# Feed-forward products on two halves of the tensor engine's rows, with the two tiles of a pair changing places

## The reference, cut to what matters

```
x = x + attention(layernorm(x), ctx)                  # 1st part of the program
n = layernorm(x)                                      # over the last axis
w_scale = mean(abs(weight))
q_w = sign(weight) * (abs(weight) > 0.5 * w_scale)    # -1, 0, 1
i_scale = max(abs(n)) / 127                           # over all of n
q_n = clip(round(n / i_scale), -128, 127)
x = x + (q_n @ q_w.T * w_scale * i_scale + bias)      # 2nd part of the program
```

## Time and profile before

| | |
|---|---|
| Time, median of 3 runs | 1268.88 us (1268.54 to 1269.37) |
| Profiled execution, own time | 1268.9 us |
| Its span, first to last instruction | 1267.0 us |
| PE busy over the span | 1201.2 us (95%) |
| DVE busy | 1124.7 us (89%) |
| ACT busy | 1001.1 us (79%) |
| Mean granted TensorE clock | 0.991 |
| Bytes read and written in HBM | 137.11 and 122.64 MB |

### The profile page before, as it was taken

How to read it: one execution, slowest core, us unless ns; L and a number is a source line. 1 busy time by engine, 2 the same in 40 slices (tenths; PEclk the granted TensorE clock), 3 DMA queues, 4 the chain that set the end, 5 groups by cost and what they waited for, 6 DMA issues and landing times.

```text
span 1267.0 us, 42077 instructions
## 1 busy us (share of the span) xinstructions
PE 1201.2 (95%) x12408; PEld 983.0 (78%) x12471; DVE 1124.7 (89%) x2410; ACT 1001.1 (79%) x2339; POOL 794.2 (63%) x1536
## 2 busy tenths in 40 slices
PE   7999999999999999999999999999789999999997
PEld 7998888888888888888888888888645555555554
DVE  4656999999999999999999999999878888888887
ACT  4566888888888888888888888888768888888886
POOL 4767898898998988989989889899700000000000
PEclk9999999999999999999999999999889999999999
DMA  9772555555555555555555543323029999999945
GB/s 291 225 205 66 160 178 169 173 173 170 164 178 166 178 168 175 170 174 162 182 163 181 164 123 94 87 84 84 2 99 398 403 396 398 399 408 396 395 206 212
DMA packets 97241, 260.26 MB, mean 205 GB/s; under 512 B 42538, under 2 KB 53994, under 8 KB 76723
## 3 DMA queue, kind: packets, MB, share of 16 engines
q1 hardware_dynamic: 97154, 259.75, 59.6%
q10 hardware_dynamic: 48, 0.07, 0.0%
HBM read 137.11 MB, written 122.64 MB: 205 GB/s over the span
## 4 chain that ended last, share of the span: by engine, by line
DVE 44%; PE 35%; issue 15%; DVEq 3%; ACT 1%; POOL 1%; DMA 0%; SPq 0%; POOLq 0%; ACTq 0%
DVE amax L903 10%; PE pT_ps L1265 10%; PE sc_ps L1265 9%; DVE x_sb L940 8%; DVE mx_sb L918 7%; DVE bn_sb L930 6%; DVE e_sb L922 6%; PE qo_ps L1069 5%; PE xT_ps L1256 5%; DVE bn_sb L910 3%; PE sc_ps L1263 2%; DVE mv_sb L947 2%; DVE rinv_sb L890 2%; PE xT_ps L1058 1%; PE pT_ps L1263 1%
## 5 line engine op out<-in xcount | busy, mean ns | idle before, releaser
L1210 PE MATMUL qo_ps<-wqs,xT_sb 128*128 128x128 f32 x2048 | 262.6, 281 | 0.9 <-ACT xT_sb L700 0.9
L1210 PEld LDWEIGHTS qo_ps<-wqs,xT_sb 128*128 128x128 f32 x2048 | 238.2, 191 | 21.5 <-issue 20.0
L1233 PEld LDWEIGHTS pT_ps<-v_blk,pT_sb 103*128 103x128 f32 x1536 | 197.3, 190 | 11.8 <-ACT pT_sb L712 0.9
L940 DVE SCALAR_TENSOR_TENSOR x_sb<-x_sb,mv_sb,xT_ps 128x512 f32 (+1 forms) x256 | 180.0, 745 | 25.5 <-DVE bn_sb L930 10.8
L1233 PE MATMUL pT_ps<-v_blk,pT_sb 103*128 103x136 f32 x1536 | 200.1, 280 | 0.3 <-ACT pT_sb L712 0.3
L1008 DVE TENSOR_TENSOR x_sb<-x_sb 128x512 f32 (+1 forms) x256 | 164.7, 684 | 1.2 <-ACT x_sb L758 1.2
L700 ACT ACTIVATE xT_sb<-xT_ps 128x512 f32<-128x512 f32 x256 | 139.1, 595 | 33.3 <-PE xT_ps L1136 28.9
L663 ACT ACTIVATE sq_sb<-x_sb 128x512 bf16 (+1 forms) x256 | 162.4, 634 | 0.6 <-DVE x_sb L940 0.2
L903 DVE TENSOR_REDUCE amax<-x_sb (+1 forms) x128 | 154.6, 1208 | 0.3 <-issue 0.3
L758 ACT ACTIVATE x_sb<-pT_ps,mean,cols 128x512 f32<-128x512 f32 x128 | 99.5, 777 | 63.6 <-PE pT_ps L1265 63.6
L1265 PE MATMUL pT_ps<-wT,x_sb 128*128 128x512 f16 x512 | 131.4, 379 | 3.2
(11 more groups left out here) (135 smaller groups left out, 2673.7 us busy)
## 6 DMA issues: line engine op xcount, KB each, us to landing
out_y<-x_sb SPq DMA_DIRECT2D x112, 1024.0 KB, 6.5
x_sb<-in_x SPq DMA_DIRECT2D x128, 512.0 KB, 3.9
x_sb<-out_y SPq DMA_DIRECT2D x48, 1024.0 KB, 8.9
x_sb<-in_ctx SPq DMA_DIRECT2D x38, 256.0 KB, 4.0
k_blk<-k_scr SPq DMA_DIRECT2D x256, 9.6 KB, 1.7
v_scr<-x_sb SPq DMA_DIRECT2D x38, 68.0 KB, 3.0
k_scr<-x_sb SPq DMA_DIRECT2D x38, 64.0 KB, 3.3
v_blk<-v_scr SPq DMA_DIRECT2D x128, 10.2 KB
```

Source lines behind the costliest of these rows:

```text
L940: dve.scalar_tensor_tensor(out=x1_at(kj, gj, t), in0=x_sb[:, kj // 2, 2 * (kj % 2) + t, :], scalar=mv_sb[:, kj, t, 0:1], in1=bank[t][:, :] ...
L1210: last = pe.matmul(bank[2][:, t * HD:(t + 1) * HD], xT_sb[:, t, c, :], wqs[:, c, :], start=c == 0, stop=c == EC - 1)
L1233: last = pe.matmul(bank[6][:, t * HEADS * VC:(t + 1) * HEADS * VC], pT_sb[0:CR, t, c * P:(c + 1) * P], v_blk[0:CR, slot, c, :, :].rearrang ...
```

## The change

PE's 128 rows are used as two halves, rows 0 to 63 (n = 0) and rows 64 to 127 (n = 1), through the feed-forward part.

- `q_T(j, m)` makes sixteen transposes of 64 rows in place of eight of 128; those of half n go to bank 2m + n. `unoffset` reads the two banks with one instruction of the same size.
- `ffn(j, m, second)` works on the pair. At first (`second` = 0) half n = 0 works on tile 2m and half n = 1 on tile 2m + 1: two bias products of 64 rows, then for each of the four chunks c one product for each half. Then (`second` = 1) the tiles change places, and the other half of the rows is added to each. Between the two, PE waits for its own first part (`ffn_half`), so that two halves never add into one bank at a time.
- `batch(j)` now runs `ffn(j, 0, 0)`, `q_T(j + 1, 0)`, `ffn(j, 0, 1)`, `ffn(j, 1, 0)`, `q_T(j + 1, 1)`, `ffn(j, 1, 1)`. The transposes stand between the two parts of a pair.
- Both tiles of a pair are done at once: `ffn_done` counts pairs, and ACT waits for it before the pair's first tile. The orders of ACT and DVE stay.
- The bias rows are copied to rows 64 to 72 by two more DVE instructions before `bias_ready`; the wait for `quant_01` and `quant_23` is on a counting register.

```diff
             def scale_out(g, k, back):
                 j = g * XS + k
                 for t in range(TPB):
-                    act.wait_ge(ffn_done_t, 4 * j + t + 1)
+                    if t % 2 == 0:
+                        act.wait_ge(ffn_done, 2 * j + t // 2 + 1)
...
-            dve.tensor_scalar(bones[0:BR, :], ones_sb[0:BR, :], row, None, ALU.mult).then_inc(bias_ready, 1)
+            mids(dve.tensor_scalar(bones[0:BR, :], ones_sb[0:BR, :], row, None, ALU.mult))
+            dve.tensor_copy(brow[HALF:HALF + BR, :], brow[0:BR, :])
+            dve.tensor_copy(bones[HALF:HALF + BR, :], bones[0:BR, :]).then_inc(bias_ready, 1)
...
-                at_least(dve, ffn_done_t, 4 * j + 2 * m - 2)
+                at_least(dve, ffn_done, 2 * j + m - 1)
...
             def q_T(j, m):
-                pe.wait_ge(quant_23 if m else quant_01, 2 * j + 2)
                 at_least(pe, qT2_copied, 2 * j + m - 1)
+                held(quant_23 if m else quant_01, 2 * j + 2, q23_count if m else q01_count, 2)
                 for t in range(2):
                     for c in range(EC):
-                        q16 = qm_sb[:, m, t, c * P:(c + 1) * P].bitcast(F16)
-                        at0 = (t * E + c * P) // 2
-                        last = pe.transpose(bank[m][:, at0:at0 + P // 2].bitcast(F16), q16[:, ::2], ident16[:, :])
+                        for n in range(2):
+                            lo, hi, at0 = n * HALF, (n + 1) * HALF, (t * EC + c) * HALF // 2
+                            q16 = qm_sb[lo:hi, m, t, c * P:(c + 1) * P].bitcast(F16)
+                            last = pe.transpose(bank[2 * m + n][:, at0:at0 + HALF // 2].bitcast(F16), q16[:, ::2],
+                                                ident16[lo:hi, lo:hi])
                 last.then_inc(qT2_done, 1)
-            def ffn(j, t):
...
+            def ffn(j, m, second):
+                if second:
+                    pe.wait_ge(ffn_half, 4 * j + 2 * m + 2)
+                else:
+                    at_least(pe, scaled_t, 4 * j + 2 * m - 2)
+                    pe.wait_ge(qT2_copied, 2 * j + m + 1)
+                    for n in range(2):
+                        rows = slice(n * HALF, (n + 1) * HALF)
+                        pe.matmul(bank[4 + 2 * m + n][:, :], bones[rows, :], brow[rows, :], start=True, stop=False)
                 for c in range(EC):
-                    last = pe.matmul(bank[4 + t][:, :], q16T_sb[:, t, c, :], wT[:, c, :], start=False,
-                                     stop=c == EC - 1)
-                last.then_inc(ffn_done_t, 1)
+                    for n in range(2):
+                        rows, t = slice(n * HALF, (n + 1) * HALF), 2 * m + (n ^ second)
+                        last = pe.matmul(bank[4 + t][:, :], q16T_sb[rows, t, c, :], wT[rows, c, :], start=False,
+                                         stop=second == 1 and c == EC - 1)
+                        if c == EC - 1 and not second:
+                            last.then_inc(ffn_half, 1)
+                if second:
+                    last.then_inc(ffn_done, 1)
...
             def batch(j, more=True):
                 for m in range(2):
-                    for t in range(2):
-                        ffn(j, 2 * m + t)
+                    ffn(j, m, 0)
                     if more:
                         q_T(j + 1, m)
+                    ffn(j, m, 1)
```

More of the change, by code:

```diff
@@ L281, in build @@
                              "scale_ready", "bias_ready"))
-        quant_01, quant_23, qT2_done, qT2_copied, ffn_done_t, scaled_t, sum_done_t = (
-            sem(n) for n in ("quant_01", "quant_23", "qT2_done", "qT2_copied", "ffn_done_t", "scaled_t", "sum_done_t"))
+        quant_01, quant_23, qT2_done, qT2_copied, ffn_half, ffn_done, scaled_t, sum_done_t = (
+            sem(n) for n in ("quant_01", "quant_23", "qT2_done", "qT2_copied", "ffn_half", "ffn_done", "scaled_t", "sum_done_t"))
         def at_least(eng, s, n):
@@ L991, in _ @@
                                           op0=ALU.mult, op1=ALU.add))
-            dve.tensor_scalar(bones[0:BR, :], ones_sb[0:BR, :], row, None, ALU.mult).then_inc(bias_ready, 1)
+            mids(dve.tensor_scalar(bones[0:BR, :], ones_sb[0:BR, :], row, None, ALU.mult))
+            dve.tensor_copy(brow[HALF:HALF + BR, :], brow[0:BR, :])
+            dve.tensor_copy(bones[HALF:HALF + BR, :], bones[0:BR, :]).then_inc(bias_ready, 1)
             def unoffset(j, m):
                 dve.wait_ge(qT2_done, 2 * j + m + 1)
-                at_least(dve, ffn_done_t, 4 * j + 2 * m - 2)
-                dve.tensor_scalar(q16T_sb[:, 2 * m:2 * m + 2, :, :],
-                                  bank[m][:, :].bitcast(F16).rearrange("p (t c r) -> p t c r", t=2, c=EC),
+                at_least(dve, ffn_done, 2 * j + m - 1)
+                ps = (xT_ps, qo_ps)[m]
+                dve.tensor_scalar(q16T_sb[:, 2 * m:2 * m + 2, :, :].rearrange("p t c (n r) -> p (t c) n r", n=2),
+                                  ps[:, :, 0:E // 2].bitcast(F16).rearrange("p n (b r) -> p b n r", r=HALF),
                                   -HALF_OFFSET, None, ALU.add).then_inc(qT2_copied, 1)
@@ L1246, in _ @@
               .then_inc(scale_row, 1)
+            q01_count, q23_count = pe.alloc_register("q01_count"), pe.alloc_register("q23_count")
+            pe.reg_mov(q01_count, 6)
+            pe.reg_mov(q23_count, 6)
             def q_T(j, m):
-                pe.wait_ge(quant_23 if m else quant_01, 2 * j + 2)
                 at_least(pe, qT2_copied, 2 * j + m - 1)
+                held(quant_23 if m else quant_01, 2 * j + 2, q23_count if m else q01_count, 2)
                 for t in range(2):
                     for c in range(EC):
-                        q16 = qm_sb[:, m, t, c * P:(c + 1) * P].bitcast(F16)
-                        at0 = (t * E + c * P) // 2
-                        last = pe.transpose(bank[m][:, at0:at0 + P // 2].bitcast(F16), q16[:, ::2], ident16[:, :])
@@ L1257, in q_T @@
-                last.then_inc(qT2_done, 1)
-            def ffn(j, t):
-                pe.wait_ge(qT2_copied, 2 * j + t // 2 + 1)
-                at_least(pe, scaled_t, 4 * j + t - 3)
-                pe.matmul(bank[4 + t][:, :], bones[:, :], brow[:, :], start=True, stop=False)
-                for c in range(EC):
-                    last = pe.matmul(bank[4 + t][:, :], q16T_sb[:, t, c, :], wT[:, c, :], start=False,
-                                     stop=c == EC - 1)
-                last.then_inc(ffn_done_t, 1)
+                        for n in range(2):
[3 more added lines that the diff above has]
+                                                ident16[lo:hi, lo:hi])
```

## The result

The changed kernel takes 1363.04 us (median of 4 runs, 1362.09 to 1364.62) against 1268.89 us before (1268.54 to 1269.37): ratio 1.0743, 95% interval 1.0724 to 1.0762. The forecast was 1382 us in a range of 1340 to 1440. The span of the profiled execution is 1362.8 us, its mean granted clock 0.981.

A forecast was written before the change was run, and what follows sets the result against it. PE was taken to bound the feed-forward part at 5.21 us a batch, then a loop through ACT at 7.01. 1268.9 + 111.6 (62 batches) + 1.1 = 1381.6, said as 1382 us, range 1340 to 1440.

The forecast's parts named there:

- S: PE's second half-products of a tile pair in the feed-forward part: four pairs of products, forecast 0.864 us.
- F: PE's first half-products of a tile pair in the feed-forward part: five pairs with the bias, forecast 1.08 us.
- Rival C: Feed-forward products: halves don't run side by side for 16-bit products of 512 columns; +174 us, 1556 us; chance 0.03.
- step 1: PE's feed-forward products: halves in different banks run side by side, 0.216 us a pair; a tile pair 1.94 us, before 2.16.
- The loop over ACT: Feed-forward batches 1 to 62: PE's products, ACT's two scalings and two quantises, PE's transposes in a ring, 7.01 us a batch.
- S1: PE's second half-products of pair 1 in a batch, forecast 0.864 us; ACT's scaling waits for them.
- Q0: PE's transposes of the next batch's pair 0, forecast 0.52 us; they wait for ACT's quantise.
- step 2: PE's feed-forward transposes: sixteen of 64 rows at 0.0325 us each, 0.52 us a group, before 0.445; bounds 0.22 and 0.90.
- Q: One group of sixteen 64-row transposes on PE for a pair of the next batch, forecast 0.52 us.
- rival B: PE's clock falls in the loop's waits: +80 us if one batch in three, +239 in all; over 50 us, chance 0.09.
- Rival A: PE's transposes: weight loads in a line, 0.90 us a group, 47 us more, 1429 us; chance 0.07.
- D: Feed-forward part: PE stays the bound at 4.93 us a batch, so faster, 1251 us; chance 0.04.

The follow-up runs named there:

- e7: Kernel before with only ACT's order altered, quantising between tiles 1 and 2 for the batch after next: 1268.73 us, ratio 0.9999.
- e1: Changed kernel with only ACT's order altered, quantising between tiles 1 and 2 for the batch after next: 1252.50 us, ratio to before 0.9878.
- e2: Changed kernel with the transposes put back behind the pair's last product, halves kept: 1304.37 us, ratio to before 1.0284.
- e6: e1's kernel with whole 128-row transposes and the unoffset of before, products still by halves: 1270.43 us, ratio to before 1.0015.
- e3: Kernel before with only the transposes made by halves (changed q_T and unoffset, old ffn): 1283.61 us, ratio to before 1.0119.

## Why the prediction was right, and where not

- PE bound the part before: e7 agrees (no gain from ACT's order alone). The 0.31 us to spare for ACT are read from the rows of before; no run tests them.
- Halves run side by side (0.216 us for a pair): right for 16-bit products of 512 columns, 0.87 us for S and 1.08 for F. Rival C (no side by side) did not come. In step 1 the rows of L1233 that I compared with as "full" have 103 rows, not 128.
- The loop over ACT is the new bound: right, and shown by e1 and e2. Its place, its 62 turns, and PE's 2 us wait in each (2.1 forecast) were as written. PE's busy share is 68% and not the 73% that I wrote: my own terms give 4.93 of 7.01 us, 70%.
- The loop's length was 6.60 us at the full clock in ACT's loop, for 7.01. Term by term, measured for forecast: S1's end to ACT 0.40 for 0.31; two scalings and two quantises 2.67 for 2.70; ACT's end to Q0 0.24 for 0.15; products 2.81 for 2.81; the two groups of transposes 0.49 for 1.04. The step that was mis-sized is step 2: Q at 0.0325 us a transpose, where it is 0.24/16 = 0.015. I took the distance of the f32 transposes of the same shape; 16-bit ones take half of that, and the low bound of 0.22 us was nearly right. This is 0.55 us a batch, 34 us.
- Two terms pull the other way: the two wake-ups (+0.18 us a batch, 11 us) and the falls of the clock (12 us), which I had as rival B and not in the sum. The batches written out, at 6.43, take off 3 us.
- The 62 intervals add up to 419.1 us for the 434.6 of the forecast, 15.5 us less. The profiled execution took 1364.6 us, 17.0 less than 1381.6; the other 1.5 us lie at the part's start and end and were not taken apart.
- Rival B happened in a small measure: 7 falls in 62 intervals, 1.65 us each. The first part's rows were the better guide here. The falls lie 3, 7, 7, 8, 7 and 7 intervals apart, so they are fairly regular. Why it falls in one batch and not in the next of the same shape is open; so is why none fell in the first 15, which are 0.17 us shorter.
- Rival A did not come: the loads of 64 rows, 16 within 0.32 us, are no bound.

```profile
1102.38 0.32 PEld L1265 LDWEIGHTS xT_ps<-ident,x_sb 64*128 64x128 f16 x16 [2.51 <-issue]
```

- D needed ACT's quantise 2 us sooner. Nothing in the change gave that, but e1 does, and there the time falls below before's, to 1252.5 us, about the 1251 that D was priced at. That the two times agree is in part luck: its pace was better than D's (4.46 us for 4.93, the transposes again), and the DMAs took the rest back. The last nine intervals are longer by 10 us in all, and the last writes end 26 us after PE (1224.5 to 1250.6 us), where before it was 6 us.

## What to carry to other kernels

When one engine's work is moved earlier, look at what it reads and where that stands in its maker's order: here the transposes went 0.9 us ahead and their input stayed behind the scaling of the last tile, with 0.31 us to spare. A change that is worth 0.75 us a batch on the bound engine cost 1.4 until one step moved on another engine. And after each gain, read the queue that was hidden before: here first ACT's, then SyncE's.

## What the runs showed of the hardware that I had not expected

- 16-bit transposes of 64 rows and 64 columns, alternating between the halves, start 0.015 us apart (16 in 0.24 us), half the distance of f32 ones of the same shape (0.0325).
- A passage between work on 128 and on 64 rows costs TensorE 0.10 to 0.11 us (e6: 0.43 us for the four in a batch); one of e3's four cost 0.35 us.
- Idle stretches of 2.05 us, with 4.6 us of work between them, were enough for the clock to fall to 1.2 GHz in 7 of 44 intervals; with stretches of 1.87 us it fell in none of 17.
- In its loop, where the numbers it waits for are held in registers, ScalarE starts 0.17 us later after the same products than in the batches written out (1.26 for 1.09 us). Whether the register is the cause was not tested.
